# Attention over two bands in one core: keys streamed once, the narrow band masked by GpSimd from memory, and a new order of the work

## The reference, cut to what matters

```python
# t: (8, 256, 128), tokens by channels, normalised before q, k, v; 8 heads of 16
scores = jnp.einsum('bhnd,bhmd->bhnm', q, k) * scale
dist = jnp.abs(idx[:, None] - idx[None, :])
for ws in (9, 17):
    mask = dist <= ws // 2
    masked = jnp.where(mask[None, None], scores, max_neg)
    attn = jax.nn.softmax(masked, axis=-1)
    out = out + jnp.einsum('bhnm,bhmd->bhnd', attn, v)
out = out / 2
t = t + out @ proj_w.T + proj_b
t = t + (qdq(ln(t)) @ qdq(ffn_kernel) + bias)
```

## Time and profile before

| | us |
|---|---|
| median of 3 runs (lowest to highest) | 106.75 (106.66 to 107.17) |
| profiled execution | 106.25 |
| its span | 104.5 |
| busy in the span: PE / DVE / ACT / POOL | 87.1 / 77.4 / 63.5 / 56.3 |

### The profile page before, as it was taken

How to read it: one execution, slowest core, us unless ns; L and a number is a source line. 1 busy time by engine, 2 the same in 40 slices (tenths; PEclk the granted TensorE clock), 3 DMA queues, 4 the chain that set the end, 5 groups by cost and what they waited for, 6 DMA issues and landing times.

```text
span 104.5 us, 4371 instructions
## 1 busy us (share of the span) xinstructions
PE 87.1 (83%) x1825; PEld 65.7 (63%) x1825; DVE 77.4 (74%) x283; ACT 63.5 (61%) x174; POOL 56.3 (54%) x118
## 2 busy tenths in 40 slices
PE   0799786999997999999999999989979757777260
PEld 0485474877775888797688788658849536444120
DVE  0011528199999999999999999999999895736221
ACT  1524556679584649974967956994996644162520
POOL 6810202057593944939799296789649464630300
PEclk9999999999999999999999999999999975555555
DMA  0725400000000000000010010000101010010101
GB/s 22 205 49 170 157 0 0 6 0 0 9 3 0 9 0 6 0 6 0 6 56 0 0 56 3 6 6 0 50 6 56 0 55 5 6 50 0 50 0 50
DMA packets 3971, 2.90 MB, mean 28 GB/s; under 512 B 944, under 2 KB 3952, under 8 KB 3952
## 3 DMA queue, kind: packets, MB, share of 16 engines
q1 hardware_dynamic: 3728, 2.56, 7.8%
q10 hardware_dynamic: 224, 0.07, 0.3%
HBM read 1.57 MB, written 1.05 MB: 25 GB/s over the span
## 4 chain that ended last, share of the span: by engine, by line
PE 55%; DVE 27%; POOL 8%; issue 3%; ACT 2%; DMA 2%; DVEq 0%
PE bank L309 10%; PE bank L323 5%; PE bank L331 5%; PE bank L300 4%; PE bank L257 4%; PE bank L266 4%; PE bank L252 4%; PE bank L274 3%; DVE row_max L791 3%; PE bank L293 3%; DVE z_sb L780 3%; PE bank L289 3%; DMA phi_w<-in_L_conv_w_phi_dram 2%; PE bank L272 2%; PE bank L294 2%
## 5 line engine op out<-in xcount | busy, mean ns | idle before, releaser
L309 PE MATMUL bank<-k_pad,q_four 64*64 64x64 f32 x512 | 17.4, 220 | 1.2 <-ACT q_four L548 1.1
L309 PEld LDWEIGHTS bank<-k_pad,q_four 64*64 64x64 f32 x512 | 15.8, 135 | 3.1 <-ACT q_four L548 1.8
L1122 POOL TENSOR_TENSOR prob<-expd,row_inv 128x256 f32<-128x256 f32 x16 | 9.9, 616 | 9.8 <-DVE row_inv L806 9.8
L323 PEld LDWEIGHTS bank<-prob_t,v_win 32*32 32x32 f32 x1024 | 10.9, 110 | 5.2 <-issue 2.7
L1116 POOL TENSOR_TENSOR diff<-narrow,row_max 128x192 f32<-128x192 f32 x16 | 8.2, 514 | 10.3 <-DVE row_max L791 10.3
L323 PE MATMUL bank<-prob_t,v_win 32*32 32x32 f32 x1024 | 12.7, 199 | 1.0 <-DVE prob_t L810 1.0
L548 ACT ACTIVATE q_four<-bank,four_mask 128x256 f32<-128x256 f32 x32 | 12.6, 483 | 0.0
L791 DVE TENSOR_REDUCE row_max<-bank 128x16 f32<-128x512 f32 x16 | 10.7, 671 | 2.1 <-ACT narrow L555 2.1
L1097 POOL TENSOR_TENSOR rstd<-ve,minus_half 128x2 f32<-128x2 f32 x8 | 5.6, 701 | 11.9 <-DVE ve L774 11.8
L555 ACT COPY narrow<-bank 128x192 f32<-128x192 f32 x16 | 5.1, 318 | 8.0 <-PE bank L309 8.0
L1129 POOL TENSOR_TENSOR prob<-prob,narrow_prob 128x192 f32<-128x192 f32 x16 | 9.5, 594 | 0.5
(11 more groups left out here) (116 smaller groups left out, 213.2 us busy)
## 6 DMA issues: line engine op xcount, KB each, us to landing
x_all<-in_x_dram SPq DMA_DIRECT2D x8, 128.0 KB, 3.8
out_dram<-out_all SPq DMA_DIRECT2D x8, 128.0 KB, 1.7
qkv_rows<-in_L_attn_qkv_w_dram SPq DMA_DIRECT2D x1, 192.0 KB, 2.6
proj_rows<-in_L_attn_proj_w_dram SPq DMA_DIRECT2D x1, 64.0 KB, 2.7
ffn_k<-in_L_ffn_kernel_dram SPq DMA_DIRECT2D x1, 64.0 KB, 2.2
proj_bias<-in_L_attn_proj_b_dram SPq DMA_DIRECT2D x1, 64.0 KB, 4.4
theta_w<-in_L_conv_w_theta_dram SPq DMA_DIRECT2D x1, 32.0 KB, 2.0
phi_w<-in_L_conv_w_phi_dram ACTq DMA_DIRECT2D x1, 32.0 KB, 2.4
```

The costliest lines, as they stand in the source:

```text
L309: last = mm(ps_scores[g][q, w, :, :], q_four[q, u % SLOTS, g * WB + w, :, :].rearrange("p e q -> p (e q)"), k_pad[q, u % SLOTS, at:at + KW ...
L323: last = mm(ps_pv[q, at:at + QUAD], v_win[q, u % SLOTS, g * WB + w, :], prob_t[q, u % SLOTS, g, w, :], start=True, stop=True)
L1122: p.tensor_tensor(prob[:, u % SLOTS, g], wide_part(expd, u, g), row_inv[:, u % SLOTS, g, 0].unsqueeze(2).to_broadcast([C, WB, KW]), ALU.mult)
```

## The change

1. `scores` streams the 32 keys once; the bank holds 256 numbers, the wide band. `lay_mask` streams 256 columns instead of 512, and `key_mask` loses the narrow half.
2. The narrow mask becomes a small table: `spread_narrow` (TensorE, one matmul at the start) and `keep_narrow_mask` (ScalarE) lay it out as `narrow_mask`, 128x24.
3. `copy_narrow` copies the unmasked inner columns to `near`. A new step `mask_narrow` (GpSimd, 16 times) adds the mask and writes `narrow`, and a new step `narrow_max` (VectorE, 16 times) takes its maximum from there. `band_max` reads 256 numbers instead of 512.
4. `subtract_narrow` waits for `narrow_max` instead of `band_max`.
5. The lists of calls of all four engines are in another order.

```diff
+            def spread_narrow():
+                pe.wait_ge(masks_made, 1)
+                pe.wait_ge(weight_done, 3)
+                mm(bank[6][:, C:C + NW], query_sel[:, :, :].rearrange("p h q -> p (h q)"), narrow_rows[:, :],
+                   start=True, stop=True).then_inc(weight_mm, 1)
...
                 wait(pe, diff_done[g], u)
-                mm(bank[4 + g][:, :], query_sel[:, :, :].rearrange("p h q -> p (h q)"),
-                   key_mask[:, g:g + WB, :, :].rearrange("p w k n -> p (w k n)"), start=True, stop=False)
...
-                        last = mm(ps_scores[g][q, w, :, :],
+                        last = mm(ps_scores[g][q, w, :],
                                   q_four[q, u % SLOTS, g * WB + w, :, :].rearrange("p e q -> p (e q)"),
-                                  k_pad[q, u % SLOTS, at:at + KW].unsqueeze(1).to_broadcast([SIDE, KINDS, KW]),
+                                  k_pad[q, u % SLOTS, at:at + KW],
                                   start=False, stop=(w == WB - 1))
...
             project_v(0)
+            spread_narrow()
             project_kq(0)
             apply_bilinear(3)
+            project_g(2)
             turn_z(1)
-            project_g(2)
             scores(0, 0)
             scores(0, 1)
...
+            def keep_narrow_mask():
+                act.wait_ge(weight_mm, 5)
+                nc.scalar.copy(narrow_mask[:, :], bank[6][:, C:C + NW]).then_inc(mask_kept, 1)
...
             def copy_narrow(u, g):
                 act.wait_ge(scores_mm[g], u + 1)
-                nc.scalar.copy(narrow[:, u % SLOTS, g], ps_scores[g][:, :, 1, INSET:INSET + NW]).then_inc(narrow_kept[g], 1)
+                nc.scalar.copy(near[:, u % SLOTS, g], ps_scores[g][:, :, INSET:INSET + NW]).then_inc(narrow_kept[g], 1)
...
             def band_max(u, g):
                 dve.wait_ge(narrow_kept[g], u + 1)
-                v.tensor_reduce(row_max[:, u % SLOTS, g], ps_scores[g], AX.X, ALU.max).then_inc(max_done[g], 1)
+                v.tensor_reduce(row_max[:, u % SLOTS, g, 0], ps_scores[g], AX.X, ALU.max).then_inc(max_done[g], 1)
 
             def subtract_max(u, g):
                 dve.wait_ge(max_done[g], u + 1)
-                v.tensor_tensor(wide_part(diff, u, g), ps_scores[g][:, :, 0, :],
-                                row_max[:, u % SLOTS, g, :, 0].unsqueeze(2).to_broadcast([C, WB, KW]),
+                v.tensor_tensor(wide_part(diff, u, g), ps_scores[g],
+                                row_max[:, u % SLOTS, g, 0].unsqueeze(2).to_broadcast([C, WB, KW]),
                                 ALU.subtract).then_inc(diff_done[g], 1)
+
+            def narrow_max(u, g):
+                dve.wait_ge(narrow_made[g], u + 1)
+                v.tensor_reduce(row_max[:, u % SLOTS, g, 1], narrow[:, u % SLOTS, g], AX.X, ALU.max).then_inc(nmax_made[g], 1)
...
+            def mask_narrow(u, g):
+                if u == 0:
+                    pool.wait_ge(mask_kept, 1)
+                pool.wait_ge(narrow_kept[g], u + 1)
+                p.tensor_tensor(narrow[:, u % SLOTS, g], near[:, u % SLOTS, g],
+                                narrow_mask[:, :].unsqueeze(1).to_broadcast([C, WB, NW]), ALU.add).then_inc(narrow_made[g], 1)
+
             def subtract_narrow(u, g):
-                pool.wait_ge(max_done[g], u + 1)
+                pool.wait_ge(nmax_made[g], u + 1)
                 p.tensor_tensor(narrow_part(diff, u, g), narrow[:, u % SLOTS, g],
-                                row_max[:, u % SLOTS, g, :, 1].unsqueeze(2).to_broadcast([C, WB, NW]),
+                                row_max[:, u % SLOTS, g, 1].unsqueeze(2).to_broadcast([C, WB, NW]),
                                 ALU.subtract).then_inc(ndiff_done[g], 1)
```

More of the change, by code:

```diff
@@ L889, in _ @@
-            subtract_max(1, 1)
-            row_sums(1, 0)
-            turn_probs(0, 1)
-            row_inverse(1, 0)
             column_max(4)
             stats_first(3)
+            subtract_max(1, 1)
+            narrow_max(1, 1)
             aggregate_first(3)
+            row_sums(1, 0)
             variance_first(3)
+            turn_probs(0, 1)
+            quantise_parts()
+            norm_first(3)
+            row_inverse(1, 0)
+            column_inverse(4)
             row_sums(1, 1)
+            pick_odd(0)
@@ L898, in _ @@
             row_inverse(1, 1)
+            window_values(2)
             band_max(2, 0)
-            norm_first(3)
-            pick_odd(0)
             turn_probs(1, 0)
-            window_values(2)
             residual(0)
+            band_max(2, 1)
+            stats_second(0)
+            narrow_max(2, 0)
+            subtract_max(2, 0)
+            stats_first(4)
+            column_max(5)
+            aggregate_first(4)
+            aggregate_second(0)
+            narrow_max(2, 1)
+            variance_first(4)
@@ L905, in _ @@
             turn_probs(1, 1)
[L906 to L908 removed]
+            row_sums(2, 0)
             subtract_max(2, 1)
[L910 to L913 removed]
             variance_second(0)
[L915 to L920 removed]
@@ L921, in _ @@
             row_inverse(2, 0)
             norm_first(4)
+            column_inverse(5)
+            quantise_join()
+            pick_odd(1)
+            turn_probs(2, 0)
+            row_sums(2, 1)
             window_values(3)
+            row_inverse(2, 1)
+            narrow_max(3, 1)
+            residual(1)
             quantise_tiny(0)
+            stats_second(1)
             column_max(6)
-            quantise_join()
-            turn_probs(2, 0)
-            row_inverse(2, 1)
-            quantise_half(0)
@@ L963, in _ @@
+            turn_probs(3, 1)
+            variance_first(6)
+            narrow_max(4, 1)
+            row_sums(4, 0)
+            result(1)
+            subtract_max(4, 1)
             row_inverse(4, 0)
-            aggregate_first(6)
-            column_max(7)
-            variance_first(6)
-            result(1)
+            norm_first(6)
+            aggregate_second(2)
+            pick_odd(3)
             row_sums(4, 1)
-            aggregate_second(2)
+            variance_second(2)
             row_inverse(4, 1)
-            variance_second(2)
@@ L984, in _ @@
+            band_max(5, 1)
             stats_second(3)
             aggregate_first(7)
+            turn_probs(4, 1)
             variance_first(7)
             row_sums(5, 0)
+            narrow_max(5, 1)
+            subtract_max(5, 1)
             aggregate_second(3)
+            quantise_tiny(2)
+            norm_first(7)
+            variance_second(3)
             row_inverse(5, 0)
-            variance_second(3)
-            quantise_tiny(2)
+            pick_odd(4)
             quantise_half(2)
+            window_values(6)
@@ L993, in _ @@
             row_sums(5, 1)
-            pick_odd(4)
+            result(2)
             row_inverse(5, 1)
-            norm_first(7)
-            window_values(6)
-            result(2)
+            residual(4)
+            turn_probs(5, 0)
+            band_max(6, 1)
             band_max(6, 0)
-            band_max(6, 1)
-            turn_probs(5, 0)
+            subtract_max(6, 0)
+            turn_probs(5, 1)
+            narrow_max(6, 0)
+            quantise_tiny(3)
             subtract_max(6, 1)
-            residual(4)
@@ L1004, in _ @@
-            subtract_max(6, 0)
             stats_second(4)
-            quantise_tiny(3)
-            turn_probs(5, 1)
+            quantise_half(3)
+            aggregate_second(4)
+            narrow_max(6, 1)
+            variance_second(4)
+            result(3)
             row_sums(6, 0)
-            quantise_half(3)
+            pick_odd(5)
             row_inverse(6, 0)
             row_sums(6, 1)
-            aggregate_second(4)
             row_inverse(6, 1)
-            variance_second(4)
```

403 lines of the change are left out of this document (208 added, 195 removed).

## The result

| us | before | after |
|---|---|---|
| median of the runs (lowest to highest) | 106.85 (106.66 to 107.17), 4 runs | 108.59 (108.08 to 109.13), 4 runs |
| profiled execution | 106.25 | 108.55 |
| its span | 104.5 | 106.8 |
| VectorE / GpSimd busy | 77.4 / 56.3 | 75.4 / 64.6 |

The ratio after to before is 1.016, with an interval of 1.0105 to 1.0217. I had forecast 106.4 and a range up to 108.5. In a second series of twelve runs the changed kernel scattered from 106.4 to 112.1, the longer ones at a lower granted clock; ratios in this document compare the undisturbed runs of each kernel alone, and medians count all runs.

What follows compares the result with a forecast made beforehand. VectorE and TensorE were taken as both full from 30 to 70 us. Masks -0.5, VectorE 0, scores 0, GpSimd +0.3 and +0.5, start +0.4, tail -1.0 sum to -0.3 us: forecast 106.4 us, range 104.5 to 108.5.

Steps and rivals of the forecast that it cites:

- The score matmuls: TensorE's score records: moving columns halve but weights stay, so the pace of 31 ns a record is unchanged; saving 0.
- The masks: `lay_mask` on TensorE streams 256 columns less, 1.7 us over 16; only VectorE's idle time can be won: -0.5 us.
- VectorE's own work: On VectorE, 256- and 192-element maxima, together 0.57 us, replace one 512-element maximum costing 0.59; taken as 0.
- GpSimd's mask: 16 `mask_narrow` of 0.51 us on GpSimd; `narrow_max` waits on them little, as masks lead: +0.3 us in the middle.
- GpSimd comes late: Rival: VectorE waits at `narrow_max` and the variances, 30 to 80 us; +2.1 over forecast, 108.5 us; chance 0.25.
- Shared-port stalls: VectorE's variance instructions, reading two memory inputs, are held up more beside a busier GpSimd: +0.5 us.
- The start: First narrow difference waits behind a second bank's mask, 0.7 us later, delaying `copy_kq(1)` and unit 1's scores: +0.4 us.
- The tail: From `row_inverse(6, 1)` on: last reciprocal 2.0 us sooner on VectorE, 1.0 given back afterwards; net -1.0 us.
- What is given back: End of the tail: `turn_z2(6)`, `quantise_tiny(6)` and `quantise_half(6)` join the path, `result(6)` leaves it: +1.0 us.
- The order's terms: The start's +0.4 us and the tail's net -1.0 us.

Runs made afterwards that it cites:

- the hybrid: Old steps; each engine's list in the old order up to what had started at 72 us, then in the changed order: 107.51 us, ratio 1.007.
- the order alone: The steps of the kernel before, all four engines' lists in the changed kernel's order: 107.58 us, ratio 1.008; in a second series 107.59 us, 1.012.

## Why the prediction was wrong

By its own steps:

- **The score matmuls, 0: right.** Two banks take 1.99 to 2.06 us as before (2.01), weight loads last 135 ns, and halving the stream in the kernel before gives 0.998. The moving columns don't set the pace. That the weight loads do is argued from the durations; no run changed the weights.
- **The masks, -0.5: the mechanism right, the gain not kept.** A `lay_mask` takes 0.21 us from start to start instead of 0.31, and while the clock is full the single columns lead the double ones by 0.4 us at unit 4 and 0.6 at unit 7. A dip of the clock takes back 1.3 or 3.1 us. I had treated TensorE's clock in the middle as given, because the earlier trace rows show 1.00.
- **VectorE's own work, 0: right.** 401 and 333 ns against the scale that I took (0.38 and 0.34 us), and taking the split away changes nothing (1.010 against 1.012).
- **GpSimd's mask, +0.3: right in its smallness, the price of one too low.** A mask takes 589 ns, my upper end, and VectorE waits 0.3 us for them in all; with and without it the ratio is 1.012 and 1.010. The rival "GpSimd comes late", which named 108.5, gives the right number by luck, for the wrong reason: its sign, VectorE at 93% or less from 30 to 70 us with waits on the masked part, came half true. VectorE is at 91%, and it waits for projections, as it does (92%) in the old steps in the new order, where no mask is on GpSimd.
- **Shared-port stalls, +0.5: the wrong sign.** `variance_second` takes 161 ns instead of 260, and the stalls of before are gone (below). As VectorE was no longer full, nothing was won by it.
- **The start, +0.4: 0.6.** The scores of unit 1 start at 25.76, 6.1 us after those of unit 0 and not 5.5. The key copy came where I had said (23.88, less the shift of 0.4, for my 23.5); that VectorE's idle time would take up a part was wrong, since TensorE stood still for the 0.67 us until `q_four` was there. And the mask isn't the only cause: without any mask, in the old steps in the new order, unit 1 comes 6.0 us after unit 0. There `band_exp(0, 0)` stands directly behind `column_exp(3)`, which the new order puts ahead of it and which was not in my sum.
- **The tail, -1.0: this is the step that failed.** It said that the first reciprocal moves to 79.03 "at the same throughput". The throughput was not the same. I had counted what stands ahead of the reciprocal on VectorE and taken its waits from the trace of before, where there are none between 74 and 78 us. But `residual` had moved forward on VectorE, to where its projection is not ready: 1.05 us, and 0.25 at `result`, in the hybrid where only the last third is new. In the whole new order the waits lie further ahead: with the old steps VectorE's waits from 30 to 82 us sum to 3.2 us, 2.1 of it at `residual`, where before has 0.7 in all. So the span between the two reciprocals shrank about as forecast (8.20), but by work and waits that now stand ahead of it and were not saved. Counted from the first scores, the last transpose comes 0.1 to 0.3 us sooner in the order alone and 0.3 in the hybrid, and 0.5 later in the changed kernel with its dip, where I had said 2.0 sooner. What is given back was sized about right: 1.0 us in the old steps (14.1 against 13.1) and 1.3 in the changed kernel, where I had taken `result(6)` off the path, but `turn_t2(7)`, and behind it `add_bias(7)`, wait for it (0.4 in the hybrid, with its clock full again for some 4 us). So the term measures +0.7 by the runs of the hybrid (1.007), of which its trace shows 0.2, and not -1.0; the traces of the order alone, its start included, show 0.7 and 0.9 behind the first scores.

The order's terms, +0.4 - 1.0 = -0.6, stand against +0.9 to +1.3 measured (1.008 and 1.012). That gap of 1.5 to 1.9 us is most of the 2.2 between forecast and result. The rest is likely the clock, whose dip in the profiled run alone cost 1.3 us; the intervals don't separate it from the small terms.

## What to carry over

When calls are reordered on two engines that are both full, check for each cross-engine pair how far the producer now stands ahead of the consumer, over the whole program: here work was moved behind a milestone and saved nothing, as a wait turned up ahead of it. The full engine's idle time by producer, before and after, is the first view to compare. And a term that makes TensorE's streams shorter is priced at full clock only; look at the granted clock of several runs before it is counted as won.

## What the runs showed that was not expected

VectorE got 16 instructions and lost 2.0 us of busy time. Most of it comes from small instructions that once ran beside GpSimd. First before, then the changed kernel (line, count, busy us, mean ns):

```profile
L737 DVE TENSOR_SCALAR k_tiny<-ffn_kc 128x128 fp8e4<-128x128 f32 x1 | 0.6, 634 | 0.0
L735 DVE TENSOR_SCALAR ffn_kc<-ffn_ks 128x128 f32<-128x128 f32 x1 | 0.5, 546 | 0.0
```
```profile
L754 DVE TENSOR_SCALAR k_tiny<-ffn_kc 128x128 fp8e4<-128x128 f32 x1 | 0.2, 226 | 0.0
L752 DVE TENSOR_SCALAR ffn_kc<-ffn_ks 128x128 f32<-128x128 f32 x1 | 0.2, 219 | 0.0
```

The same instruction takes 634 ns or 226 by where it stands. With `k_half` (523, 226), `lift` (497, 171) and the eight variances (0.8 us) that is 2.1 us. The Trainium skill ("SBUF — State Buffer", section "Who interferes with whom") says that VectorE's tensor-with-scalar operations can, in a mode that reads memory through two ports, take the port pair that is shared with GpSimd, and that whichever of the two issues first then blocks the other for its whole instruction. The traces agree: the excess of 408 ns is below the 510 to 600 ns of one GpSimd instruction. Before, `k_tiny` ran from 30.87 to 31.50 us beside a sum on GpSimd from 30.83 to 31.42; now it stands at 34.37, where GpSimd is idle (34.05 to 35.61). Not every GpSimd instruction does this: `lift`, at 33.70, took 171 ns wholly beside a `rstd` of 2 columns that lasted from 33.34 to 34.05.

Two profiles can start their first scores 0.5 us apart (19.3 and 19.8) with equal lists up to there. 0.2 of it is the wait of the first matmul for its loads (3.2 and 3.4 us); the rest isn't traced. A term of half a microsecond in the start can't be read from one profile.
